# A four-layer graph-attention kernel on one core: the start of the first layer reordered, its first source row spread by TensorE, the row factors made later

## The reference, cut to what matters

```python
h = einsum('nf,hfd->hnd', x, W)                # 4 heads of 64
s_src = einsum('hnd,hd->hn', h, a[:, :64, 0])
s_dst = einsum('hnd,hd->hn', h, a[:, 64:, 0])
e = leaky_relu(s_src[:, :, None] + s_dst[:, None, :], 0.01)
e = where(adj[None] == 0, -inf, e)
out = elu(einsum('hij,hjd->hid', softmax(e), h))
```

## Time and profile before

| | us |
|---|---|
| runs (three) | 3138.89, 3136.37, 3134.41; median 3136.37 |
| profiled execution | 3136.09 |
| its span | 3134.3 |
| TensorE busy | 2962.0 (95%) |
| VectorE busy | 2157.9 (69%) |
| ScalarE busy | 1910.1 (61%) |
| GpSimd busy | 1156.1 (37%) |

### The profile page before, as it was taken

How to read it: one execution, slowest core, us unless ns; L and a number is a source line. 1 busy time by engine, 2 the same in 40 slices (tenths; PEclk the granted TensorE clock), 3 DMA queues, 4 the chain that set the end, 5 groups by cost and what they waited for, 6 DMA issues and landing times.

```text
span 3134.3 us, 65810 instructions
## 1 busy us (share of the span) xinstructions
PE 2962.0 (95%) x24616; PEld 2583.8 (82%) x24616; DVE 2157.9 (69%) x3878; ACT 1910.1 (61%) x3389; POOL 1156.1 (37%) x1542
## 2 busy tenths in 40 slices
PE   6789999999979999999997999999999999879997
PEld 5789999999959999999996887887778778645554
DVE  3898888887779888888776555665665665652244
ACT  3667898999969999999984444454455444420000
POOL 0282365652125556564122023333323333524212
PEclk9899999999989999999998999999999999999999
DMA  8456200000100000000010000000000000000000
GB/s 302 154 208 234 74 11 14 11 14 14 59 15 12 13 12 13 11 13 11 14 33 15 4 1 4 4 1 4 1 4 4 1 1 1 3 1 0 0 20 33
DMA packets 42335, 105.25 MB, mean 34 GB/s; under 512 B 9904, under 2 KB 23472, under 8 KB 33968
## 3 DMA queue, kind: packets, MB, share of 16 engines
q1 hardware_dynamic: 42160, 102.92, 9.8%
HBM read 98.51 MB, written 4.39 MB: 33 GB/s over the span
## 4 chain that ended last, share of the span: by engine, by line
PE 75%; DVE 4%; ACT 2%; issue 2%; POOL 1%; DMA 0%; POOLq 0%; DVEq 0%; SPq 0%; ACTq 0%
PE bank L1189 16%; PE bank L1186 16%; PE bank L1238 15%; PE bank L1276 12%; PE bank L1192 11%; PE bank L1265 2%; PE bank L1252 1%; PE bank L1146 1%; ACT above L856 1%; PE bank L1382 0%; DVE lnst L1527 0%; ACT rings L981 0%; DVE x L1517 0%; DVE values L1514 0%; DVE x L1540 0%
## 5 line engine op out<-in xcount | busy, mean ns | idle before, releaser
L1186 PE MATMUL bank<-values,rings 128*128 128x195 bf16 x8192 | 1413.8, 247 | 57.1 <-DVE rings L1775 53.0
L1189 PE MATMUL bank<-values,rings 128*128 128x195 bf16 x8192 | 1413.9, 249 | 0.0
L856 ACT ACTIVATE above<-srow,kpass 128x512 fp8e4<-128x512 f32 x2048 | 1291.8, 709 | 179.2 <-DVE rings L1775 173.5
L1186 PEld LDWEIGHTS bank<-values,rings 128*128 128x128 fp8e4 x8192 | 806.3, 98 | 67.8 <-issue 65.8
L1189 PEld LDWEIGHTS bank<-values,rings 128*128 128x128 fp8e4 x8192 | 788.7, 96 | 0.5
L1770 DVE TENSOR_TENSOR rings<-rings,above 128x512 uint32<-128x512 uint32 x512 | 399.3, 780 | 208.3 <-PE bank L1189 188.4
L934 ACT ACTIVATE values<-srow,cmul 128x512 f32<-128x512 f32 x256 | 206.0, 814 | 432.7 <-PE bank L1276 431.9
L1775 DVE TENSOR_TENSOR rings<-rings 128x512 uint32<-128x512 uint32 x512 | 429.9, 840 | 17.2
L1276 PE MATMUL bank<-hv,values 128*128 128x257 f32 x1792 | 423.0, 381 | 10.2 <-DVE values L1636 10.2
L1276 PEld LDWEIGHTS bank<-hv,values 128*128 128x128 f32 x1792 | 336.3, 191 | 80.9 <-issue 25.5
L1192 PE MATMUL bank<-values,rings 128*128 128x390 bf16 x2048 | 341.0, 328 | 19.1 <-DVE values L1573 19.1
(11 more groups left out here) (197 smaller groups left out, 3418.4 us busy)
## 6 DMA issues: line engine op xcount, KB each, us to landing
arena<-in_adj_dram SPq DMA_DIRECT2D x64, 1024.0 KB, 5.2
srow<-src_dram SPq DMA_DIRECT2D x72, 256.0 KB, 3.1
x<-in_x_dram SPq DMA_DIRECT2D x1, 4096.0 KB, 14.6
out_dram<-x SPq DMA_DIRECT2D x8, 512.0 KB, 2.9
arena<-in_L_gnn_fe_w_dram SPq DMA_DIRECT2D x2, 512.0 KB, 7.1
arena<-in_L_gnn_W_hz_dram SPq DMA_DIRECT2D x1, 1024.0 KB, 7.8
arena<-in_L_gnn_g_w_dram SPq DMA_DIRECT2D x1, 1024.0 KB, 11.0
weights<-in_L_gnn_W_dram SPq DMA_DIRECT2D x3, 256.0 KB, 4.0
```

Of the source, the lines that this page charges most:

```text
L856: last = act.activation(above[:, k % 2, q, :], srow[:, par, :], ACT.Relu, scale=BIG, bias=kpass[:, p % 2, k * Q + q:k * Q + q + 1], satura ...
L1186: pe.matmul(acc[:, 0:KW], pos[:, k % 2, q, :].bitcast(FP8)[:, rows], v[:, 0:KW], start=start, stop=final, skip_group_check=True)
L1189: last = pe.matmul(acc[:, KW:2 * KW], neg[:, k % 2, q, :].bitcast(FP8)[:, rows], v[:, KW:2 * KW], start=False, stop=final, skip_group_chec ...
```

## The change: what it does

- x is loaded in four pieces of 1 MB, each with its own semaphore; TensorE waits for a piece before quads 0, 2, 4 and 6. ScalarE's queue issues layer 0's weights. TensorE waits for the fold only after the first quad's transposes.
- Seven tiles are packed in front of attention: tiles 0 to 4 one quad later than before (after the products of quads 1 to 5), tiles 5 and 6 after `src_rows`. VectorE stores those two in group 0. The other 25 go three to a group in eight groups and one in the ninth.
- `FRONT` takes (1, 0) as the fifth group, (1, 1) as the ninth and (0, 7) as the tenth. GpSimd waits for ten groups instead of nine before the values of pass 2.
- In layers 0 and 1 TensorE transposes a broadcast column of scores four times into bank 5, which gives the first source row on all partitions; ScalarE copies it into `srow`. The first row is no longer read from DRAM.
- In layers 0 and 1 VectorE makes `kscores` right after the shifted scores and signals. ScalarE takes two exps instead of three before `s_exps`. The row factors' five VectorE instructions stand in unit 0 of group 0, their exp after `above` of unit 1. In unit 0 ScalarE makes two of the four `above` before the first casts.

```diff
-PACKED_FIRST = QUADS
+PACKED_FIRST = 7
+X_PIECES = 4
+PACKED_WOVEN = 5
-FRONT = [(0, 0), (0, 1), (0, 2), (0, 3), (0, 4), (1, 0), (0, 5), (0, 6), (0, 7), (1, 1)]
+FRONT = [(0, 0), (0, 1), (0, 2), (0, 3), (1, 0), (0, 4), (0, 5), (0, 6), (1, 1), (0, 7)]
 PACKS = 3
+def packed_before(at):
+    return min(PACKED_FIRST + at * PACKS, T)
 def packs_of(at):
+    return range(packed_before(at), packed_before(at + 1))
...
 # SyncE
-                load(0, 0)
                 load(1, NG * FRONT[1][0] + FRONT[1][1] if l == 0 else 1)
...
-            sp.dma_start(x[:, :, :], A["x"].rearrange("(t p) f -> p t f", p=P)).then_inc(s_x, 16)
-            load_weights(0)
+            for i in range(X_PIECES):
+                piece = slice(i * (T // X_PIECES), (i + 1) * (T // X_PIECES))
+                sp.dma_start(x[:, piece, :], A["x"].rearrange("(t p) f -> p t f", p=P)[:, piece, :]).then_inc(s_x[i], 16)
+            for s in range(2):
+                for hd in range(H):
+                    load_vector(avec[:, s, hd * D:(hd + 1) * D], A["L0_gnn_a"][hd, s * D:(s + 1) * D, 0])
...
 # GpSimd, front()
+                    if at == 0:
+                        pool.wait_ge(s_rowexp, 1)
                     quotient(0, p, g, at % 2, at)
-                pool.wait_ge(s_unit, (NG + 1) * BITS + CREDIT)
-                for g in range(2):
-                    values_of(0, 2, g)
-                for g in range(1, NG):
-                    if g > 1:
-                        values_of(0, 2, g)
+                pool.wait_ge(s_unit, len(FRONT) * BITS + CREDIT)
+                values_of(0, 2, 0)
+                quotient(0, *FRONT[-1], 1, len(FRONT) - 1)
+                values_of(0, 2, 1)
+                for g in range(2, NG):
+                    values_of(0, 2, g)
                     quotient(0, 1, g, g % 2)
...
 # ScalarE, stats(l)
+                if l < 2:
+                    act.wait_ge(s_rowps, l + 1)
+                    act.activation(srow[:, 0, :], bank[5][:, :], ACT.Copy).then_inc(s_srow[0], 16)
...
-                    act.activation(e[:, 0], e[:, 0], ACT.Exp)
-                    act.activation(c, c, ACT.Exp).then_inc(s_exps, 1)
+                    act.activation(e[:, 0], e[:, 0], ACT.Exp).then_inc(s_exps, 1)
+            def row_factors(l):
+                act.wait_ge(s_rowshift, 4 * (l + 1))
+                c = cmul[:, :, :, :].rearrange("p k h t -> p k (h t)")
+                act.activation(c, c, ACT.Exp).then_inc(s_rowexp, 1)
 # ScalarE, group(), first group
                     if k > 0:
                         above_of(k, range(Q))
+                    else:
+                        row_there()
+                        above_of(k, (0, 1))
...
-                        row_there()
-                        above_of(k, range(Q))
+                        above_of(k, (2, 3))
                         above_of(k + 1, range(Q))
+                        row_factors(l)
...
+            for k in range(2):
+                act.dma_start(weights[:, k, 0:F].rearrange("p (h d) -> p h d", h=H),
+                              A["L0_gnn_W"][:, k * P:(k + 1) * P, :].rearrange("h p d -> p h d")).then_inc(s_w, 16)
 # TensorE
+                if q == 0:
+                    pe.wait_ge(s_wfix, l + 1)          # in dense(), after the transposes
...
+                if l < 2:                              # in src_rows()
+                    for it in range(GT):
+                        last = pe.transpose(bank[5][:, it * P:(it + 1) * P],
+                                            scores[:, 0, it:it + 1].to_broadcast([P, P]), ident[:, :])
+                    last.then_inc(s_rowps, 1)
...
-                    pe.wait_ge(s_wfix, l + 1)
                     for q in range(QUADS):
+                        if l == 0 and q % (QUADS // X_PIECES) == 0:
+                            pe.wait_ge(s_x[q // (QUADS // X_PIECES)], 16)
                         dense(l, q)
-                        if l == 0:
-                            pack(q)
+                        if l == 0 and 1 <= q <= PACKED_WOVEN:
+                            pack(q - 1)
                     src_rows(l)
+                    if l == 0:
+                        for t in range(PACKED_WOVEN, PACKED_FIRST):
+                            pack(t)
 # VectorE
+                if l < 2:                              # in stats(), after the shifted scores
+                    dve.tensor_scalar(kscores[:, :, :], dst, BIG, None, ALU.mult).then_inc(s_shift, 1)
+                    dve.wait_ge(s_exps, l + 1)
+                    return
...
+                    if l == 0 and first and k == 0:    # in group(), after first_products
+                        store_packed(PACKED_WOVEN, 6 + PACKED_WOVEN % 2)
...
+                        if first and k == 0:           # after first_rests
+                            row_factors(l)
...
+                        if l == 0 and first and k == 0:    # after neg of unit 0
+                            store_packed(PACKED_WOVEN + 1, 6 + (PACKED_WOVEN + 1) % 2)
-                        if k < 2 * PACKS:
+                        if k < 2 * len(packs_of(g)):
                             convert(packs_of(g)[k // 2], k % 2)
```

More of the change, by code:

```diff
@@ L55 @@
 TURN = {0: 0, 1: 1, 3: 2}
-FRONT = [(0, 0), (0, 1), (0, 2), (0, 3), (0, 4), (1, 0), (0, 5), (0, 6), (0, 7), (1, 1)]
+FRONT = [(0, 0), (0, 1), (0, 2), (0, 3), (1, 0), (0, 4), (0, 5), (0, 6), (1, 1), (0, 7)]
 PACKS = 3
-PACKING = (T - PACKED_FIRST) // PACKS
+def packed_before(at):
+    return min(PACKED_FIRST + at * PACKS, T)
 def packs_of(at):
-    return range(PACKED_FIRST + at * PACKS, PACKED_FIRST + (at + 1) * PACKS) if at < PACKING else ()
-def packed_before(at):
-    return PACKED_FIRST + min(at, PACKING) * PACKS
-assert all(packed_before(at) >= (g + 1) * GT for at, (p, g) in enumerate(FRONT)) and packed_before(PACKING) == T
+    return range(packed_before(at), packed_before(at + 1))
+assert all(packed_before(at) >= (g + 1) * GT for at, (p, g) in enumerate(FRONT))
 PASSES = {0: H, 1: H, 3: H // 2}
@@ L287, in gnn_kernel @@
         src_dram = [nc.dram_tensor(f"src_dram{l}", [H * T, P], F32)[:, :] for l in range(3)]
-        s_x = sem("x_loaded")
+        s_x = [sem(f"x_loaded{i}") for i in range(X_PIECES)]
         s_w = sem("weights_loaded")
@@ L313, in gnn_kernel @@
         s_srcps = sem("src_in_psum")
+        s_rowps = sem("first_row_in_psum")
         s_src = sem("src_transposed")
@@ L318, in gnn_kernel @@
         s_shift = sem("shifts_made")
+        s_rowshift = sem("row_shifts_made")
+        s_rowexp = sem("row_factors_made")
         s_exps = sem("exps_made")
@@ L369, in load_weights @@
             def load_weights(l):
-                if l == 0:
-                    for k in range(2):
-                        sp.dma_start(weights[:, k, 0:F].rearrange("p (h d) -> p h d", h=H),
-                                     A["L0_gnn_W"][:, k * P:(k + 1) * P, :].rearrange("h p d -> p h d"))\
-                            .then_inc(s_w, 16)
-                    for s in range(2):
-                        for hd in range(H):
-                            load_vector(avec[:, s, hd * D:(hd + 1) * D], A["L0_gnn_a"][hd, s * D:(s + 1) * D, 0])
-                    return
                 sp.dma_start(weights[:, :, 0:F], A[f"L{l}_gnn_W"].rearrange("(k p) f -> p k f", p=P))\
@@ L428, in score_rows @@
                     for at in range(1, len(FRONT) - 1):
-                        for t in packs_of(at - 1):
+                        for t in (*packs_of(at - 1), *(packs_of(at) if at == len(FRONT) - 2 else ())):
                             if t > PACKED_FIRST:
@@ L670, in attention @@
                     chain.settle()
+                    if l == 1 and p == 0:
+                        pool.wait_ge(s_rowexp, 2)
                     with pool.Fori(0, NG // 2 - 1) as gg:
@@ L824, in stats @@
                 act.wait_ge(s_shift, l + 1)
-                e, c = (m[:, :, :, :].rearrange("p k h t -> p k (h t)") for m in (emul, cmul))
+                e = emul[:, :, :, :].rearrange("p k h t -> p k (h t)")
                 if l == 2:
@@ L1743, in group @@
                         words = packed[:, :, front * WORDS:(front + 1) * WORDS]
-                    if front is not None and g > 0 and packs_of(g - 1) and k == 0:
-                        store_packed(packs_of(g - 1)[PACKS - 1], GT * par + PACKS - 1)
+                    if front is not None and g > 0 and k == 0:
+                        if len(packs_of(g - 1)) == PACKS:
+                            store_packed(packs_of(g - 1)[PACKS - 1], GT * par + PACKS - 1)
                         dve.wait_ge(s_packed, packed_before(g) + CREDIT)
@@ L1784, in group @@
                             summed.then_inc(s_banksum, 1)
-                    if front is not None and packs_of(g):
-                        if k < 2 * PACKS:
+                    if front is not None:
+                        if l == 0 and first and k == 0:
+                            store_packed(PACKED_WOVEN + 1, 6 + (PACKED_WOVEN + 1) % 2)
```

(12 more changed lines are left out.)

22 lines of the change are left out of this document (9 added, 13 removed).

## The result

The changed kernel took 3126.59 us (median of 7 runs, 3124.97 to 3126.92), the kernel before, beside it, 3136.51 (7 runs). The ratio is 0.9965, 95% interval [0.9955, 0.9974]: 9.9 us gone, where 11.1 were forecast (3125.3 against the 3136.4 of the first three runs). The profiled execution is 3125.94, span 3124.1.

A forecast was written before the change was run, and what follows sets the result against it. TensorE, busy 95% of the span, was taken as the bound, with VectorE pacing some groups; only TensorE's idle or slowly clocked time could go. -10.4 + 1.8 - 2.3 = -10.9 from 3136.09 gave 3125.2, stated as 3125.3; range 3121 to 3131 us.

The forecast's parts named there:

- fold starts: Layer 0's start: VectorE's fold of weights and avec begins at 17.3 us instead of 19.81, saving 2.55 us.
- first products to the next quad: Layer 0's first quad: 5.5 us from the fold's end, its transposes having run in the idle time before.
- maximum: Layer 0: VectorE takes the maximum of the scores near 71.4 us, within 0.2 us of the last score copy.
- maximum to first matmul, layer 0: From the maximum of the scores to attention's first matmul: 10.4 us instead of 12.44, set by ScalarE's chain.
- the same, layer 1: The same stretch in layer 1: 10.2 us instead of 12.46, so 2.3 us saved.
- store of tile 6: In the groups, VectorE's store of tile 6 stands behind the first `neg` and adds 0.6 us.
- tile 31: Packed in the ninth group, where TensorE paces: one pack, 1.8 us more, between nothing and 2.5.
- ahead at layer 1's first matmul: The changed kernel's lead over the kernel before when layer 1's attention starts: 10.9 us, the whole sum.
- bound from x landing first: Layer 0's loads: served in order, avec lands no earlier than x, so the fold is done no earlier than 19.3 us.
- slower start: Layer 0's first quad: TensorE's lower clock after standing still falls on the products, giving 0.9 us back.
- (B): Layer 0's loads: avec lands at 19 as before, the fold comes no earlier, costing 2.5 us: 3127.8 us; chance 0.13.
- (C): Fifth group: (1, 0) waits for GpSimd's values, 2 to 5 us lost, about 3129 us; chance 0.12.
- (D): Fifth group: the same GpSimd wait but long; 15 us late gives about 3139 us; chance 0.05.

The follow-up runs named there:

- c1: The changed kernel again with nothing edited, as a control: 3126.92 us, 10.7 below the kernel before.
- e2: Changed kernel with the two weight DMAs back on SyncE, between the x pieces and avec: 3127.0 us.
- e3: Changed kernel with x loaded in one 4 MB DMA instead of four pieces: 3126.02 us.
- e1: Changed kernel with SyncE issuing the eight avec DMAs ahead of the four x pieces: 3122.74 us.
- e8: Changed kernel with the row factors ahead of `kscores` again in layers 0 and 1, and their exp ahead of VectorE's products: 3129.39 us.
- e10: Changed kernel with (1, 0) taken as the fourth group instead of the fifth: 3146.30 us.
- e9: Changed kernel with the first source row over DRAM again, without the row transposes and row copy; two `above` still ahead of the casts: 3133.18 us.
- e5: Changed kernel with all four `above` of unit 0 behind the first four casts again, in layers 0 and 1: 3128.60 us.
- e7: Changed kernel with all seven tiles packed beside the quads, none after the scores and none stored in group 0: 3129.44 us.
- e4: e1 with the conversion of tile 6's second half moved behind the row factors in unit 0 of group 0: 3120.79 us.
- e11: e4 with tiles 0 to 4 packed behind quads 2 to 6 instead of 1 to 5: 3118.70 us.
- e12: e11 with the conversion of tile 6's first half also behind the row factors in unit 0 of group 0: 3121.02 us.

## Why the prediction was right, step by step

The mechanism held, and the direction of every term. By terms, forecast against the trace (c1 in brackets):

| step | forecast | measured |
|---|---|---|
| fold starts | 17.3 | 18.33 (18.50) |
| first products to the next quad | 5.5 | 5.36 (5.57) |
| maximum | 71.4 | 72.33 (72.71) |
| maximum to first matmul, layer 0 | 10.4 | 10.32 (10.32) |
| the same, layer 1 | 10.2 | 10.05 (10.09) |
| store of tile 6 | +0.6 | +0.61 (+0.59: 9.84 ahead at the first matmul, 9.25 at group two) |
| tile 31 | +1.8 | +0.5 (+0.7) |
| ahead at layer 1's first matmul | 10.9 | 10.83 (11.14) |
| sum, by the spans | -10.9 | -10.2 (-11.5) |

*The fold* is the term mis-sized. I freed 2.5 us of SyncE's queue; 1.5 came (1.3 in c1). By e2 moving the weights is worth 1.6 to 1.85; with them on SyncE the three more x pieces cost 0.4 (fold at 20.18 against 19.81), with them on ScalarE nothing (e3). Avec landed at 18.3, 1.7 us after the last of x (issued at 3.5, landed 13.1 us later), so the bound from x landing first held. What I did not ask was why avec stood behind x at all: by e1 its place in the queue cost 10 us, more than all that was changed there.

*First quad and quads.* The slower start did fall on the products: their 16 took 5.52 us, against 4.74, so 0.8 us were given back where 0.9 were forecast. That this is the lower clock is read from e8, where the granted clock is 0.50 (1.2 GHz) from 14 to 26 us, while TensorE stands and then starts its products, and 1.00 (2.4 GHz) from 27. The view of the change's trace gives 1.00 for this stretch, but there too the scores of one tile follow those of the last by 1.62 us at first (24.66, 26.28) and by 0.89 after. The slow stretch ends at a different place each time: the same 16 products took 5.25 us (e10) to 6.86 us (e9), so 0.8 is one draw out of 0.5 to 2.1.

*From the maximum on* the step by step sum over ScalarE was within 0.1 us in layer 0 and 0.15 in layer 1. Its bounds, 1.5 to 3.5 us a layer, were too narrow for its own sum, which took 3.9 for layer 0 from the last score on; measured are 4.0 (14.37 before, 82.65 - 72.30 now). The parts are shown: `above` ahead of the casts 1.26 and 0.89 (e5), the row that allows it (e9), row factors 1.5 a layer (e8), two packs in the gap (e7). In layer 1 the 0.89 and 1.55 of e5 and e8 make up the 2.41 by which the gap shrank; in layer 0 1.26 and 1.50 are more than its 2.12. There VectorE also stores tile 5 within the gap now; what that costs was not tested. VectorE was 0.67 us from being the bound, which e4 ran into.

*Tile 31* seems to have cost less than its pack row, but this term was not measured alone, since the order of groups changed in the same stretch. Between the ninth group's start and layer 1's maximum the kernel before takes 926.11 - 339.65 = 586.46 us, the change 586.98 and c1 587.16. In the first 60 us of that TensorE had 0.84 us idle before and 0.16 after, by the windows; that accounts for 0.7 of the 1.8, the rest was not looked into.

*The rivals.* (B) fell: the fold came 1.5 us sooner. (C) had its mechanism and not its size: TensorE waits for GpSimd's last value at the fifth group in c1 and nine more of the experiments' traces (e2 to e5, e7 to e9, e11 and e12), 1.0 us each time, of which 0.5 counts in c1. The 0.6 us of slack was 2.3 us in the change's first trace and -0.5 in c1. That the forecast did not need this wait in its sum is in part luck: it was safe by less than it scatters. (D)'s cliff is real but one group away: e10 stands on it.

## What to carry to other kernels

Ask of the first wait not which engine should issue the load, but what lies ahead of it in its queue: eight small DMAs put ahead of 4 MB gave 8.65 us at the first product, and moving the weights to another queue 1.6 to 1.85 at the fold. Then look for what is late next; of those 8.65 us 3.1 reached the maximum, because the adjacency, which came no sooner, had become the bound, and an instruction that waited for it stood in front of one that did not. And take a second trace of the same kernel before explaining a difference between single groups of work: here they differed by 2.8 us and then came within 0.9. For the same reason compare each median with the kernel before of its own batch: that kernel's own median moved by 2.4 us between batches.

## What the runs showed of the hardware that was not expected

- Issuing small DMAs takes longer behind a large load, whichever DMA is next: 9.64 us for the weights, 6.35 and 6.80 us for x pieces and avec in the change, 13.12 us for avec behind one x (e3), 3.72 us for avec with nothing ahead (e1). That the engine stands because its queue is full is a reading, which no run tests.
- GpSimd stops for 10.33 to 10.58 us ahead of its first product of values in every trace (and 112.76 to 123.11 in the change), wherever group 0 ends; the cost is the same each time, and no run here shows its cause.
